# Loading each expert's input tile one step ahead instead of two in a fused Mamba and mixture-of-experts layer

## The reference

```python
logits = x @ gate_w
top_v, top_i = jax.lax.top_k(logits, K)              # K = 2 of E = 8
top_p = jax.nn.softmax(top_v, axis=-1)
combine = jnp.zeros((T, E)).at[arange(T)[:, None], top_i].add(top_p)
g = jnp.einsum('th,ehi->tei', x, Wg)                 # h = 256, i = 704
u = jnp.einsum('th,ehi->tei', x, Wu)
d = jnp.einsum('tei,eih->teh', jax.nn.silu(g) * u, Wd)
expert_out = jnp.einsum('te,teh->th', combine, d)
shared = jax.nn.silu(x @ Sg) * (x @ Su) @ Sd
return (expert_out + shared).reshape(b, s, h)
```

## Time and profile before

| | |
|---|---|
| median of three runs | 1845.75 us |
| the profiled execution's own time | 1850.68 us |
| its span, first to last instruction | 1849.1 us |
| phase 2, first load to the end | 1203.4 to 1849.1 us |
| mean granted TensorE clock | 0.951 |

### The profile page before, as it was taken

How to read it: one execution, slowest core, us unless ns; L and a number is a source line. 1 busy time by engine, 2 the same in 40 slices (tenths; PEclk the granted TensorE clock), 3 DMA queues, 4 the chain that set the end, 5 groups by cost and what they waited for, 6 DMA issues and landing times. The chain is left out here.

```text
span 1849.1 us, 23292 instructions
## 1 busy us (share of the span) xinstructions
PE 1594.4 (86%) x6828; PEld 1030.2 (56%) x6828; DVE 1172.0 (63%) x1953; ACT 859.0 (46%) x1498; POOL 1039.0 (56%) x1192
## 2 busy tenths in 40 slices
PE   5788798898998998998997685478999999999990
PEld 2344555554644645645555454356777777777770
DVE  1298999898999898998989993122222222222225
ACT  3566658567667567576575562111212212122124
POOL 0568778778778788788788872312222222222224
PEclk9899999999999999999999887689999999999996
DMA  3111112111211121111112111178212222122116
GB/s 94 47 35 47 47 45 84 64 55 43 70 52 47 64 59 46 64 58 53 52 47 69 41 46 47 58 257 260 35 32 33 33 35 33 33 35 33 33 30 187
DMA packets 82983, 115.65 MB, mean 63 GB/s; under 512 B 10992, under 2 KB 56912, under 8 KB 82864
## 3 DMA queue, kind: packets, MB, share of 16 engines
q1 hardware_dynamic: 61552, 81.33, 14.1%
q0 software_dynamic: 17088, 28.65, 7.7%
q10 hardware_dynamic: 4224, 4.19, 0.7%
HBM read 81.05 MB, written 33.10 MB: 62 GB/s over the span
## 5 line engine op out<-in xcount | busy, mean ns | idle before, releaser
L894 POOL TENSOR_TENSOR bb<-u,br 128x512 f32<-128x512 f32 x512 | 646.4, 1274 | 183.0 <-DVE hh L749 180.7
L615 ACT ACTIVATE bA<-dt,a_neg 128x512 f32<-128x512 f32 x512 | 353.5, 692 | 294.7 <-DVE hh L749 289.2
L480 PEld LDWEIGHTS bH<-ident,hh 128*128 128x128 f32 x2048 | 254.4, 146 | 304.0 <-issue 154.8
L480 PE MATMUL bH<-ident,hh 128*128 128x128 f32 x2048 | 324.6, 284 | 74.7 <-DVE hh L749 60.4
L749 DVE TENSOR_TENSOR_SCAN hh<-bA,bb 128x512 f32<-128x512 f32 x256 | 306.5, 1210 | 46.4 <-ACT bA L615 36.0
L749 DVE TENSOR_TENSOR_SCAN hh<-bA,hl,bb 128x512 f32<-128x512 f32 x256 | 322.5, 1271 | 17.7 <-ACT bA L615 17.7
L766 DVE SCALAR_TENSOR_TENSOR yT<-bH,bc,yT 128x512 f32<-128x512 f32 x360 | 262.8, 730 | 35.0 <-PE bH L480 34.4
L1260 POOL DMA_INDIRECT sum_scratch<-yt,xt x71 | 113.3, 1595 | 189.2 <-issue 151.5
L1295 ACT ACTIVATE sgm<-bG 128x352 f32<-128x352 f32 x142 | 58.1, 461 | 326.6 <-PE bG L1120 326.6
L1163 PE MATMUL bD<-w_d,hT 128*128 x852 | 198.4, 383 | 0.8 <-ACT hT L1301 0.8
L1254 POOL DMA_DIRECT2D xt<-expert_in_scratch x71 | 40.6, 572 | 273.3 <-PE bX L1152 191.4
(11 more groups left out here) (176 smaller groups left out, 1961.9 us busy)
## 6 DMA issues: line engine op xcount, KB each, us to landing
br<-b_scratch SPq DMA_DIRECT2D x128, 256.0 KB, 3.2
xt<-expert_in_scratch POOLq DMA_DIRECT2D x71, 132.0 KB, 2.4
w_g<-in_L_ffn_Wg_dram SPq DMA_DIRECT2D x8, 704.0 KB, 4.3
w_u<-in_L_ffn_Wu_dram SPq DMA_DIRECT2D x8, 704.0 KB, 6.1
w_d<-in_L_ffn_Wd_dram SPq DMA_DIRECT2D x8, 640.0 KB, 7.8
xp<-in_L_attn_x_dram SPq DMA_DIRECT2D x8, 512.0 KB, 4.9
xr<-in_L_attn_x_dram SPq DMA_DIRECT2D x8, 512.0 KB, 4.9
x_scratch<-xr SPq DMA_DIRECT2D x8, 512.0 KB, 3.2
```

The costliest lines, as they stand in the source:

```text
L480: i = e.transpose(bH[g % NH][:, q * P:(q + 1) * P], hh[:, (n - 1) % 2, q, d * P:(d + 1) * P], ident[:])
L615: e.activation(bA[g % NA][:], dt[c % 2][:, d, :], ACT.Exp, scale=a_neg[:, d, n:n + 1]).then_inc(s_a, 1)
L894: e.tensor_tensor(bb[:, k % NB, :], u[c % 2][:, d, :], br[:, n % NR, :], ALU.mult).then_inc(s_bb, 1)
```

## The change

In its iteration t GpSimd issued the load of tile t+2, and then the scatter of tile t-1. Now it issues the load of tile t+1, and then the scatter of t-1. The loop starts one iteration later, so that the same 71 loads and 71 scatters are issued. The buffers stay four. The wait on the buffer follows the tile's number: the load of tile n waits, as before, for the scatter of tile n-4.

```diff
-            for t in range(-2, NT + 1):
-                n = t + 2
-                if n < NT:
-                    if n >= NX:
-                        e.wait_ge(s_tx, n + 1 - NX)
-                        e.wait_ge(s_gt, n + 1 - NX)
-                        e.wait_ge(s_ys, 16 * (n + 1 - NX))
-                    row = e.value_load(tab[0:1, 1, n:n + 1], min_val=0, max_val=SPARE + (E - 1) * P)
-                    e.dma_start(xt[:, n % NX, :], xs_d[bass.ds(row, P), :]).then_inc(s_in[n % NX], 16)
+            for t in range(-1, NT + 1):
+                if t + 1 < NT:
+                    if t + 1 >= NX:
+                        e.wait_ge(s_tx, t + 2 - NX)
+                        e.wait_ge(s_gt, t + 2 - NX)
+                        e.wait_ge(s_ys, 16 * (t + 2 - NX))
+                    row = e.value_load(tab[0:1, 1, t + 1:t + 2], min_val=0, max_val=SPARE + (E - 1) * P)
+                    e.dma_start(xt[:, (t + 1) % NX, :], xs_d[bass.ds(row, P), :]).then_inc(s_in[(t + 1) % NX], 16)
                 if t >= 1:
                     e.wait_ge(s_in[(t - 1) % NX], 16 * ((t - 1) // NX + 1))
```

## The result

Four runs of the changed kernel took 1899.01 to 1904.16 us, median 1900.96, beside 1845.59 for the kernel before: 1.0295 times as long, 95% interval 1.027 to 1.0321, that is about 54 us slower (the medians differ by 55.4). The forecast was 1909. A fifth execution, from which the profile comes, took 1905.28 us; its span is 1903.7 us, and the granted clock is 0.951 as before.

The account below looks back on a forecast made before the run. TensorE's own work was taken to bound the kernel after 1300 us, DMA chains beside the weights before. Costs of 17.3, 44.8 and 0.75 us gave +62.9, 1908.6 against the median, forecast 1909; 8-in-10 range 1878 to 1938.

Parts of the forecast that it names:

- The rhythm: After 1300 us TensorE waits for the load in every tile; the period goes from 8.20 to 8.95 us, +0.75 a tile.
- One tile per trip: The round trip from scatter through load and TensorE to next scatter carries one tile, where before 12.2 us served two.
- The load's start at S + 1.90: S is a scatter's start; the next load starts after its 1.60 us on GpSimd plus a 0.30 us gap.
- The 0.20 us behind the scatter's packets: After 1300 us, the load's extra delay behind the adding scatter's moving packets, taken as 0.20 us between nothing and 1.33.
- From the landing to the next scatter, 4.39 us: Time from a load's landing, through TensorE's turning and down product, to the next scatter's start: 4.39 us.
- The stretch with the weights: While expert weights load, landing 8.0 us after scatter start and slow clock in half the tiles cost 17.3 us by tile 5.
- The sum: Weights' part 17.3, 62 periods +44.8 and one more waiting tile +0.75 us make +62.9 us on the whole kernel.
- The mild case: The load behind the scatter lands as if alone everywhere: period 8.70 us, +34 us, 1880; chance 0.13.
- the harsh one: The load's packets rest until the scatter has landed: period 10.1 us, 1986 us in all; chance 0.07.
- The clock: TensorE's short idle time in each tile lowers its clock after 1300 us: +80 us on top, about 1990; chance 0.03.
- The faster case: Beside the weights the load no longer waits for a scatter's landing, so up to 9.5 us return: 1836; chance 0.03.
- The two rules of the Trainium skill: Semaphore order makes the low end beside the weights some 5 us dearer; port lockout, doubted, could add up to 30 us.

## Why the prediction was right

- *The rhythm.* One tile per trip was the step from which the time was to follow, and it holds: three buffers made the trip longer and the beat with it, and shortening it in three different ways (the scatter's kind, the place of the turning, another issuing engine) brought the beat back to 8.20 to 8.29. The beat was forecast at 8.95 and is 8.94; tiles 5 to 67 take 554.4 us (1842.12 - 1287.69) for the 554.9 of the sum.
- *The load's start at S + 1.90.* Wrong: it starts at 1.07 us. The gap of 0.30 us between two DMAs doesn't hold where the second is prepared while the first is generated; the two instructions overlap in the profile, and the load's is drawn longer, 1.13 us. It ends at 2.20 us, not at 2.47. This start, and a landing more than 3 us behind it, were both named as signs that the forecast is wrong; the time stands all the same, since it hangs on the landing after S and not on where the load starts.
- *The 0.20 us behind the scatter's packets.* Too little: the runs show 0.4. Phase 1's scatters gave the wrong neighbour, for they don't add; with a scatter that writes, the load lands as if alone. The two errors, -0.27 and about +0.2, cancel by luck, and the landing, put at 4.55 and 4.51 in the mean, was right for reasons partly wrong.
- *From the landing to the next scatter, 4.39 us.* Right: 1510.42 - 1506.03 is 4.39.
- *The stretch with the weights.* The cost at tile 5 was put at 17.3 us. It is 14.4 in the profiled execution (1287.69 - 1224.35 = 63.3, for 48.9 before), but another execution of the same kernel had 53.0, 4 us. By tile 8, when both are past the weights, the cost is 15.1 and 10.3 us (90.2 and 85.4, for 75.1 before). The load was put at 8.0 us after S in every trip; it lands at 8.0, 6.7, 7.9, 4.5 and 8.3, 7.1 in the mean, so this term was too dear. Its mechanism is confirmed, also the fall of the clock after the idle stretches of 3.85 to 4.20 us, and not after that of 2.64.
- *The sum.* From the first scatter to the end the profiled execution is 59.5 us longer for the 62.9 of the forecast: +14.4, +44.3 (554.4 - 510.1), +0.8 behind tile 67, where the last waiting tile is. That the spans differ only by 54.6 is due to phase 1: its first load in phase 2 stands at 1198.36 us, and stood at 1203.37. That the medians differ by 55.4, and not by 60, fits the varying stretch beside the weights, which was long in this profile: in the second profile of the changed kernel the same piece is 55.1 us longer. 1909 was 8 us too high.
- *The rivals.* The mild case falls by the beat, 8.94 and not 8.70, and by the 0.4 us; the harsh one by the 0.4 us too, for 1.33. The clock stayed at 1.00 through the short waits after 1300 us. The faster case named the right loss, 9.5 us beside the weights, and the wrong cure: it came back with a fifth buffer and two tiles of lead, not with a shorter lead.
- *The two rules of the Trainium skill.* The one on the semaphore increment, which lands only after every earlier write of its DMA engine, stands in the Trainium skill, "DMA: Bandwidth & Descriptors", section "Queues, rings and completion order". In the first trip beside the weights the scatter lands 7.5 us after its start and the load behind it at 8.0. That agrees with the rule, but plain queueing would show the same. The one on the port that VectorE and GpSimd share (the Trainium skill, "SBUF — State Buffer", section "Who interferes with whom") costs nothing here, as the forecast had it: with VectorE's copies moved away from the load its instruction and its landing are as long as with them (1.14 and 3.4 us). That a source in PSUM keeps a copy out of the modes that take both ports is stated not by that page but by the Trainium skill's "VectorE: DVE Perf Modes", section "Why PSUM operands drop a tier"; the 1.14 and 3.4 us agree with it.

## What to carry to other kernels

Where a load stands in a queue behind a store that depends on the same engine's last result, draw the round trip and count the tiles that it carries. The lead of the load in tiles is that count, and the time per tile is the trip divided by it or the engine's own work, whichever is longer. A wait for a landing in the trip is hidden at one lead and sets the pace at the next, and a stretch with heavy traffic can make it visible where the mean doesn't; one more buffer, at two tiles of lead, won about 9 us here.

## What the runs showed of the hardware

- By the profile's records GpSimd began a load 0.53 us before the scatter ahead of it had ended (1502.50 for 1503.03), where the gap between two DMAs seen before was 0.30 us. The table read (1501.29) and the address work (until 1501.97) lie around the scatter's start at 1501.43, as their wait had been met; in the kernel before, where it was for the scatter's landing, the table read came at 1505.1.
- A scatter of 128 rows of 1 KB that adds takes 1.60 us to generate and lands 3.9 us after its start; the same one writing takes 1.01 and 2.5. A load behind the first lands about 0.4 us later than alone, counted from the end of its own instruction, behind the second not at all.
- The same load issued by SyncE lands in 2.1 us instead of 2.4.
- Idle stretches of 3.7 us in each tile kept the granted clock at 0.87 in the mean from 1350 to 2200 us; those of about 0.6 us left it at 1.00.
